# First chunk of a gated cross-attention and FFN kernel taken as two pieces of 256 rows

## The reference

```python
# 16 heads of 32
q = layernorm(x) @ Wq.T + bq                  # x: (8192, 512)
k, v = split(ctx @ Wkv.T + bkv)               # ctx: (4, 154, 512)
att = softmax(q @ k.T / sqrt(32))             # per head, over 154 keys
x = x + tanh(g_xattn) * ((att @ v) @ Wo.T + bo)
h = relu(layernorm(x) @ w1.T + b1)            # 2048 wide
out = quantize_5_10(quantize_4_3(h) @ quantize_4_3(w2).T + quantize_5_10(b2))
x = x + tanh(g_ffn) * out
```

## Time and profile before

| | us |
|---|---|
| median of three runs | 1588.99 |
| the profiled execution | 1590.96 |
| its span, first to last instruction | 1589.2 |
| PE busy | 1532.4 (96%) |
| DVE busy | 948.6 (60%) |
| ACT busy | 813.0 (51%) |
| POOL busy | 878.5 (55%) |
| mean granted TensorE clock | 0.987 |

### The profile page before, as it was taken

How to read it: one execution, slowest core, us unless ns; L and a number is a source line. 1 busy time by engine, 2 the same in 40 slices (tenths; PEclk the granted TensorE clock), 3 DMA queues, 4 the chain that set the end, 5 groups by cost and what they waited for, 6 DMA issues and landing times.

```text
span 1589.2 us, 23580 instructions
## 1 busy us (share of the span) xinstructions
PE 1532.4 (96%) x8576; PEld 692.9 (44%) x8576; DVE 948.6 (60%) x1297; ACT 813.0 (51%) x1196; POOL 878.5 (55%) x919
## 2 busy tenths in 40 slices
PE   7875999999999999999999999999999999999998
PEld 4422444444444444444444444444444444444443
DVE  7778465674756566574656657574665757445231
ACT  3665564545545564555546455554645455455421
POOL 3688365564736556474655547464654746445310
PEclk9997999999999999999999999999999999999999
DMA  8356363453544454344445444344543534333120
GB/s 335 97 158 149 116 160 110 134 119 112 111 132 104 117 135 109 105 107 149 101 116 137 116 99 115 124 103 130 134 115 103 120 113 104 102 98 86 44 54 27
DMA packets 252855, 186.70 MB, mean 117 GB/s; under 512 B 160012, under 2 KB 209476, under 8 KB 251076
## 3 DMA queue, kind: packets, MB, share of 16 engines
q1 hardware_dynamic: 252740, 185.19, 43.7%
HBM read 99.95 MB, written 51.59 MB: 95 GB/s over the span
## 4 chain that ended last, share of the span: by engine, by line
PE 75%; DVE 11%; POOL 6%; issue 5%; ACT 2%; DMA 1%; SPq 0%; DVEq 0%; ACTq 0%
PE ring L514 53%; PE ring L708 8%; PE m_ps L616 4%; DVE y L1014 4%; PE s_ps L646 2%; PE y_ps L674 2%; DVE bns L1039 2%; DVE resid L1056 2%; DVE xn L1065 1%; PE d_ps L663 1%; POOL x L1149 1%; POOL rs L1161 1%; POOL pmain L1123 1%; DMA resid<-in_w_t 1%; PE s_ps L639 1%
## 5 line engine op out<-in xcount | busy, mean ns | idle before, releaser
L514 PE MATMUL ring<-late_a,w 128*128 128x512 f16 x3072 | 703.1, 380 | 7.2 <-issue 7.2
L514 PEld LDWEIGHTS ring<-late_a,w 128*128 128x128 f16 x3072 | 299.0, 98 | 347.3 <-issue 17.4
L815 ACT ACTIVATE late_b<-ring,b_sb,wsc 128x512 fp8e4<-128x512 f32 x256 | 199.4, 779 | 396.7 <-PE ring L514 396.7
L1123 POOL TENSOR_TENSOR pmain<-p,pmain 128x512 f16<-128x512 f32 x256 | 302.0, 1182 | 176.3 <-ACT p L793 173.2
L992 DVE TENSOR_REDUCE smax<-m_ps 128x4 f32<-128x616 f32 x256 | 203.4, 794 | 226.7 <-PE m_ps L616 226.5
L1014 DVE RECIPROCAL y<-d_ps 128x256 f32<-128x256 f32 x128 | 223.4, 1745 | 64.2 <-PE d_ps L666 61.9
L793 ACT ACTIVATE p<-s_ps,prob_log,sc 128x512 f32<-128x512 f32 x320 | 247.9, 775 | 1.0 <-POOL pleft L1123 1.0
L708 PE MATMUL ring<-w,late_b 128*128 128x512 fp8e4 x1024 | 228.5, 379 | 5.6 <-DVE ffn L1023 3.8
L790 ACT ACTIVATE pmain<-s_ps,prob_log,sc 128x512 f16<-128x512 f32 x256 | 198.1, 774 | 5.9 <-PE s_ps L646 5.8
L1123 POOL TENSOR_TENSOR pleft<-p,pleft 128x512 f16<-128x512 f32 x64 | 76.5, 1195 | 182.0 <-ACT p L793 182.0
L514 PE MATMUL ring<-wo,yT 128*128 128x512 f16 x768 | 175.0, 381 | 0.0
(11 more groups left out here) (149 smaller groups left out, 1424.0 us busy)
## 6 DMA issues: line engine op xcount, KB each, us to landing
qstack<-q_rows SPq DMA_DIRECT2D x192, 128.0 KB, 3.0
pstack<-left_rows SPq DMA_DIRECT2D x192, 128.0 KB, 2.6
xin<-in_x SPq DMA_DIRECT2D x64, 256.0 KB, 3.4
q_rows<-qparts SPq DMA_DIRECT2D x32, 512.0 KB, 2.8
left_rows<-pleft SPq DMA_DIRECT2D x64, 256.0 KB, 2.5
resid<-in_x SPq DMA_DIRECT2D x64, 256.0 KB, 3.2
out_x<-resid SPq DMA_DIRECT2D x64, 256.0 KB, 2.7
resid<-in_w_t SPq DMA_DIRECT2D x5, 1024.0 KB, 6.2
```

Of the source, the lines that this page charges most:

```text
L514: last = pe.matmul(dst, lhs(a, k), rhs(b, k), start=(k == 0 and p == 0), stop=(k == n_k - 1 and p == 2))
L815: nc.scalar.activation(hT[:, j, :], ring_bank("h", c, j)[:], ACT.Relu, bias=b1_sb[:, j:j + 1], scale=wsc[:, j // 4, 1:2], saturate=False). ...
L1123: nc.gpsimd.tensor_tensor(part[:, 1, :], p32[:, n % 2, :], part[:, 0, :], ALU.subtract).then_inc(prob_lo, 1)
```

## The change

Chunk 0 is taken in two pieces: piece 0 is its tiles 0 and 1, piece 1 its tiles 2 and 3; chunk c from 1 on is piece c + 1 and stays whole. Attention, projection and FFN run by pieces. Piece 0 stands one period of 28 beats ahead of piece 1: its attention is in beats -28 to -1, piece 1's in 0 to 27, chunk 1's in 28 to 55 as before. The loop starts at beat -40 in place of -12. For a piece of 256 rows an instruction keeps its form and takes 256 columns in place of 512: lifts, exponentials, rests, values, `y_hi`, `y_lo`, hidden products, `relu`. `normalise`, which worked in halves of 256 columns, has one half per group in a piece of 256. The steps done once are moved by some 28 beats to earlier ones, the own tables of chunks 0 and 1 are written anew, and the semaphore counts go by pieces.

```diff
-FIRST, LAST = -12, 70
-MAX_OWN = {0: [-12, -11, ..., 2, 3], 1: [18, 19, 20, 21, 22, 23, 24, 25, 27, 29, 30, 30, 33, 34, 38, 39]}
-SHIFT_OWN = {0: [-4, 4], 1: [26, 42]}
-LN1_STAT_OWN = {1: [-1, 1, 3, 5]}
-Q_OWN = {1: [16, 17, 21, 27]}
-O_OWN = {0: [33, 35, 36, 37]}
-LN2_OWN = {0: [35, 36, 37, 38]}
+FIRST, LAST = -40, 70
+MAX_OWN = {0: [-40, -37, -36, -35, -33, -32, -29, -26, -25, -19, -15, -9, -5, -3, 1, 5]}
+SHIFT_OWN = {0: [-35, -24], 1: [-7, 6]}
+LN1_STAT_OWN = {1: [-13, -5, -2, 3]}
+Q_OWN = {1: [16, 18, 24, 25]}
+VALUE_OWN = {0: [-21, -13, -6, 3], 1: [10, 16, 21, 28]}
+NORMAL_OWN = {0: [-21, -18, -14, -12, -7, -2, 0, 3], 1: [7, 10, 15, 16, 21, 25, 28, 39]}
+O_OWN = {0: [5, 6, 33, 35]}
+LN2_OWN = {0: [6, 8, 34, 36]}
+X2TURN_OWN = {0: [8, 8, 38, 43]}
+HIDDEN_OWN = {0: [14, 14, 15, 16, 19, 21, 22, 23, 25, 26, 28, 29, 30, 31, 33, 34], 1: [40, 43, 43, 47, 49, 51, 51, 53, 53, 54, 54, 54, 55, 56, 60, 61]}
+FFN_OWN = {0: [37, 38, 65, 67]}
-W1_SUM = {1: -9, 2: -7, 3: -2}
-W_FOLD = {0: 1}
-W1_LO = {0: 13, 1: 26, 2: 26, 3: 38}
-W2_LOAD = {0: 27, 1: 47, 2: 49, 3: 53}
-W2_PART = {0: 43, 1: 49, 2: 52, 3: 56}
+W1_SUM = {1: -39, 2: -33, 3: -28}
+W_FOLD = {0: -29}
+W1_LO = {0: -11, 1: 4, 2: 8, 3: 9}
+W2_LOAD = {0: 2, 1: 24, 2: 30, 3: 32}
+W2_PART = {0: 17, 1: 26, 2: 32, 3: 35}
...
+        def run_pieces(stage_fn, at, b, own={}):
+            for p, beats in own.items():
+                for k, beat in enumerate(beats):
+                    if beat == b:
+                        stage_fn(p, k)
+            for k, r in enumerate(at):
+                before, rest = divmod(b - r, PERIOD)
+                if rest == 0 and 0 <= before + 1 < NCH + 1 and before + 1 not in own:
+                    stage_fn(before + 1, k)
+        def tiles_of(p):
+            return ((0, 2), (2, TILES))[p] if p < 2 else (0, TILES)
+        def rank_of(c, u):
+            if c:
+                return divmod(u, TILES)
+            p, rest = divmod(u, 2 * KT)
+            return rest // 2, 2 * p + rest % 2
...
-                product(ring_bank("h", c, j)[:], lambda a, k: w1[:, j // 4, a, k, j % 4 * P:j % 4 * P + P],
-                        lambda b, k: x2T[:, b, k, :], KT).then_inc(hid_done, 1)
+                product(ring_bank("h", p, j)[:, 0:width(p)], lambda a, k: w1[:, j // 4, a, k, j % 4 * P:j % 4 * P + P],
+                        lambda b, k: x2T[:, b, k, columns(p)], KT).then_inc(hid_done, 1)
...
-                nc.vector.reciprocal(y32[:, cols], d_ps[:, cols]).then_inc(inverted, 1)
+                if half >= halves:
+                    return
+                nc.vector.reciprocal(y32[:, cols], d_ps[:, cols]).then_inc(inverted, 2 // halves)
```

More of the change, by code:

```diff
@@ L303, in build @@
             steps_of(KV_STEPS, lambda n, k: ring_jobs.append(("kv", 0, n)) if k == 0 else None, beat)
[L304 to L306 removed]
+            for kind, at, own in (("q", Q_AT, Q_OWN), ("o", O_AT, O_OWN), ("h", HIDDEN_AT, HIDDEN_OWN),
+                                  ("f", FFN_AT, FFN_OWN)):
+                by = run_pieces if kind == "h" else run
+                by(lambda c, k: ring_jobs.append((kind, c, k)) if (kind, c) != ("q", 0) else None, at, beat, own)
         ring_place = {job: n for n, job in enumerate(ring_jobs)}
@@ L312, in ring_bank, with chunk_of, width, columns @@
             return ring[ring_place[kind, c, k] % 2]
[L314 to L318, removed]
+        def chunk_of(p):
+            return max(p - 1, 0)
+        def tiles_of(p):
+            return ((0, 2), (2, TILES))[p] if p < 2 else (0, TILES)
+        def width(p):
+            first, end = tiles_of(p)
+            return (end - first) * P
+        def columns(p):
+            first, end = tiles_of(p)
+            return slice(first * P, end * P)
+        def opens_piece(c, t):
+            return t == 0 or (c, t) == (0, tiles_of(1)[0])
+        def piece_at(c, t):
+            return c + 1 if c or t >= tiles_of(1)[0] else 0
+        def group(p, m):
+            return p * KT + m
+        def unit(p, m, u):
+            return group(p, m) * (GH + 1) + u
+        def rank_of(c, u):
[3 more added lines that the diff above has]
+            return rest // 2, 2 * p + rest % 2
+        def ranks_of(p, m):
+            return 8 * p + 2 * m + 2 if p < 2 else (p - 1) * 16 + 4 * m + 4
         def q_stage(c, m):
@@ L662, in value @@
                     for h in range(GH):
-                        pe.matmul(d_ps[DH * h:DH * h + DH, :], ones[:], pmain[:, h, part, :],
+                        pe.matmul(d_ps[DH * h:DH * h + DH, 0:w], ones[:], pmain[:, h, part, 0:w],
                                   start=(part == 0), stop=False)
                 for h in range(GH):
-                    last = pe.matmul(d_ps[DH * h:DH * h + DH, :], ones_stack[0:96, :], pstack[0:96, h, :],
+                    last = pe.matmul(d_ps[DH * h:DH * h + DH, 0:w], ones_stack[0:96, :], pstack[0:96, h, 0:w],
                                      start=False, stop=True)
@@ L729, in _ @@
                 run(project, O_AT, beat, O_OWN)
-                run(hidden, HIDDEN_AT, beat)
-                run(ffn_out, FFN_AT, beat)
+                run_pieces(hidden, HIDDEN_AT, beat, HIDDEN_OWN)
+                run(ffn_out, FFN_AT, beat, FFN_OWN)
         @block.scalar
@@ L868, in _ @@
                 run(lambda c, m: query_hi(c, m) if c else None, Q_AT, beat, Q_OWN)
-                run(relu, HIDDEN_AT, beat)
+                run_pieces(relu, HIDDEN_AT, beat, HIDDEN_OWN)
                 run(lambda c, t: x_hi(c, t) if c else None, XSPLIT_AT, beat, XSPLIT_OWN)
@@ L1070, in _ @@
             nc.vector.memset(sums[:], 0.0)
+            nc.vector.memset(smax[:], 0.0)
             link(nc.vector.memset(ones_stack[:], 0.0))
@@ L1096, in _ @@
                 run(row_max, MAX_AT, beat, MAX_OWN)
-                run(shift, SHIFT_AT, beat, SHIFT_OWN)
-                run(normalise, NORMAL_AT, beat)
+                run_pieces(shift, SHIFT_AT, beat, SHIFT_OWN)
+                run_pieces(normalise, NORMAL_AT, beat, NORMAL_OWN)
                 run(ln2_apply, LN2_AT, beat, LN2_OWN)
@@ L1102, in _ @@
                 run(residual, O_AT, beat, O_OWN)
-                run(finish, FFN_AT, beat)
+                run(finish, FFN_AT, beat, FFN_OWN)
                 run(lambda c, t: ln1_stat(c, t) if c else None, LN1_STAT_AT, beat, LN1_STAT_OWN)
```

259 lines of the change are left out of this document (133 added, 126 removed).

## The result

The changed kernel takes 1608.86 us (median of four runs, 1608.42 to 1611.21) against 1589.66 us for the kernel before in the same rounds: a ratio of 1.0124, with a 95% interval of 1.0112 to 1.0136. It is 19.2 us slower; 5.7 us faster was forecast, with a range up to 1597.

A forecast was written before the change was run, and what follows sets the result against it. PE was taken to set the pace at 92.1 us a chunk, after its late start. First lift 44.5 + fill 73.6 + PE work 119.0 + pauses 13.5 gave 250.6 against 256.3, hence 1583.3 us, range 1571 to 1597.

The forecast's parts named there:

- The first lift: Start of attention, after four ranks and the shift row instead of eight ranks: at 44.5 us, 6.9 us sooner.
- The fill: From first lift to first narrow hidden product: 73.6 us, so that product comes at 118.1 us.
- The division by 79%: In the fill: ACT's summed durations, 58.1 us, divided by DVE's earlier busy share of 79%, giving 73.6 us.
- PE's work behind it: From first narrow hidden product to chunk 1's hidden layer: 92.1 + 26.9 = 119.0 us without a pause.
- The narrow matmuls at half price: Hidden products of 256 columns: 0.108 us per matmul, half a wide one, weight loads hidden.
- The pauses: PE's waits and slow clock between first narrow hidden product and chunk 1's hidden layer: four items, 13.5 us.
- ahead of chunk 1's hidden layer: Pause there because two of four covering output products were done long before: 2.6 to 5.6 us, taken 4.5.
- ahead of piece 1's: Pause before piece 1's hidden layer, 9.3 us of cover against a longer chain: 1.3 to 4.8, taken 3.
- at `w2`: Pause from four 1 MB loads, each behind a conversion, which the last output awaits: 0 to 8 us, taken 4.
- the first products at half clock: Start of piece 0's hidden layer: first matmuls run at half clock, costing 2 us.
- rival C: Start moves but cover is lost whole: pauses at 19 us, above all beats 40 to 68; 1589 us, chance 0.17.
- the milestone: Start of chunk 1's hidden layer: 250.6 us against 256.3, 5.7 us sooner; the end moves by the same.

The follow-up runs named there:

- e1: Kernel before, with each hidden product of chunk 0 made as two products of 256 columns: 1590.08 us, ratio 0.9997.
- e4: Changed kernel, with each of the four w2 loads bringing a quarter of its bytes: 1607.37 us, ratio 1.0109.
- e9: Kernel before, with chunks 4 to 9 given hidden products and relu of 256 columns and two outputs cut to one matmul: 1544.97 us.
- single relief: On e9, chunks 4 to 11: row maxima over 8 keys, 1528.90 us; or second exponential and POOL's rest over 128 columns, 1512.34 us.
- both reliefs: Changed kernel: row maxima of chunks 1 and 2 over 8 keys; second exponential and rest over 128 columns, chunk 2 and most of chunk 1: 1600.19 us.
- e10: Changed kernel, with piece 1's hidden products placed in the beats of every other chunk: 1607.27 us, ratio 1.0109.
- e14: Changed kernel, with each hidden product of piece 1 made twice and placed in the other chunks' beats: 1617.70 us, ratio 1.0176.

## Why the prediction was wrong

**The first lift** came at 48.2 us, not 44.5. The fourth maximum was ready at 40.8 us where I had 38.5 to 39.5, the shift row was issued at 42.14, after a first instruction of 1.05 us where I had 0.2, and the lift stood in PE's order behind a rank that waited 1.56 us for a split of the queries. The row alone would have allowed about 46.

**The fill** was right to the digit, and the terms of the sums hold: 73.6 us forecast, 73.6 taken from the first lift to the first narrow hidden product; exponentials of 0.564 us for 0.56; the durations of all instructions in it add up to 58.0 us on ACT and 57.9 on DVE, for 58.1 and 57.6. The division by 79% was luck. A busy share counts the time in which instructions of an engine overlap once, a sum of durations counts it twice (two exponentials of the changed kernel in order of time):
```profile
166.61 0.77 ACT L844 ACTIVATE pmain<-s_ps,prob_log,sc 128x512 f16<-128x512 f32 x1
167.28 0.77 ACT L847 ACTIVATE p<-s_ps,prob_log,sc 128x512 f32<-128x512 f32 x1
```
In the same 73.6 us ACT was busy for 50.2 and DVE for 52.6, 68 and 72%, where 79% was forecast. So I divided a sum of one kind by a share of the other, and the fuller share that this needed and the looser fill that came cancelled. Before the first hidden product PE had waited 4.09 us for the transposes, so the last step was SP's queue, which I had not priced.

**PE's work behind it** was right: 119.0 forecast, 118.0 by count. The narrow matmuls at half price were right (e1).

**The pauses** are the step that failed: 13.5 us forecast, 33.6 measured. I named four places and priced them singly, and they came out at or near their prices: 3.42 for 4.5 us ahead of chunk 1's hidden layer, none for 3 ahead of piece 1's, 2.03 for 4 at `w2` (e4: 1.5 to 2.4 us of the time), and some 2.2 for 2 in the first products at half clock (24 narrow ones from 121.80 to 126.58 us, 4.8 us for 2.6). What I missed is that outside those places I let PE's own work set the length of the stretches. What PE would wait, or run at half clock, between them I put at nothing, and it was some 26 us. The row of the steady period showed that PE's 91.8 us cover the others' 57, 48 and 54; it did not show that 63 us would. They don't: with 64 us the period is 83.4 to 85.0 (e9), and 83.4 in the changed kernel with 63.2. My rival C named this stretch and DVE's 54 us in it, but at 19 us of pauses and a result of no change: right in kind, too small.

**The sum** then reads: first lift 3.7 us late, pauses 20.1 us more, PE's work 1.0 less, which is the 22.8 us by which the milestone was missed. The period behind it took 93.6 us where 92.1 was forecast, since its first product ran at half clock (4.2 us for 2.6); by the end 0.8 us of that is left. The median was missed by 2.0 us more, 25.6 in all: the profiled execution before had stood 2 us above its median, and the one after did not. Of the signs named beforehand, the pauses (over 20 us) and the period behind chunk 1's hidden layer speak against the prediction; the first hidden product, within 110 to 125 us, does not.

**Why the change loses at all.** The kernel before starts its first full period at 161.6 us and is never thin after. The changed one has two thin periods, 68.1 and 83.4 us, for 54.8 and 63.2 us of PE's work. It wins 13 us in PE's lost time ahead of the first hidden product (before: 161.6 us for some 93 of work by count, after: 121.8 for some 66) and loses 33.6 us behind it, where before it was some 4 (the 94.7 us to chunk 1's hidden layer held 91 of work). ACT's busy time grew by 15.9 us (813.0 to 828.9) through the narrow exponentials, `relu` and splits. 60 of the 80 narrow exponentials lie in the fill; what the others, the 32 `relu` and four splits add in the two thin stretches is some 9 us by their durations. What that costs was not tried, but e9 comes to the same floor with no narrow exponentials.

**What stays open.** Which handover sets the floor, and what part SP's queue has in it: no single relief moved it by more than 5.7 us. And the first thin stretch (68.1 us) gave only 2 us to both reliefs, so its 13.3 us lost are less explained than the 20.2 of the second. Its waits of PE inside are 7.4 us, 3.7 of them for maxima and 2.0 at `w2`; e9, e10 and e14 do not bear on it.

## What to carry to other kernels

An engine that is 99% busy at 92 us hides how long the others would take without it; their busy sums (57, 48, 54) did not tell it here, since the floor was 80 to 85. Before moving the bounding engine's work out of a stage, halve that work in a steady stage and measure what the stage takes. Splitting the first chunk brought its first hidden product 40 us forward, but left PE two thin periods that cost more than the start had gained. And where a sum of durations is divided by a busy share, both must count overlapping instructions alike.

## What the runs showed of the hardware that was not expected

Matmuls of 256 columns over full-height weights, each with a weight load of its own, ran at 0.109 us each, 36 of them in a row in 3.93 us (226.18 to 230.11 in the changed kernel), and 384 of them at no cost beyond half of the wide ones (e1). The granted clock stood at 0.94 in stretches where PE was busy for 69 of 83 us, and at 1.00 in e10, with 66 of 80 us busy. So at nearly the same busy share (83 and 82%) it ran at half clock for part of the one and at full clock for all of the other. The two differ in where the hidden products, and so the waits, stand. Successive exponentials of 0.77 us followed each other on ACT at 0.67 us; in the fill the sum of its durations, 58.0 us, is some 8 us above its busy time.
